# Context attention of a two-layer perceiver: the shifted queries are kept in the PSUM bank of the shift rows instead of in an SBUF tile

## The reference

```python
q = _ln((x @ Wq + bq).reshape(b, s1, H, HD), qn_w, qn_b)
k = _ln(kv[..., :HD], kn_w, kn_b);  v = kv[..., HD:]
ctx = _attn(qT, k.transpose(0, 2, 1, 3), v.transpose(0, 2, 1, 3))   # softmax(q k^T * SCALE) v over 1585 keys
ctx = ctx + DCA_WEIGHT * ctx_dca
return ctx @ Wo + bo
```

## Time and profile before

| | us |
|---|---|
| median of 3 runs (lowest to highest) | 3159.53 (3156.69 to 3160.48) |
| the profiled execution | 3156.05 |
| its span, first to last instruction | 3154.2 |
| PE busy | 2869.8 (91%) |
| DVE busy | 2625.1 (83%) |
| ACT busy | 2282.5 (72%) |
| POOL busy | 1615.4 (51%) |

### The profile page before, as it was taken

One profiled execution on the slowest core, in us unless ns is written; L12 is line 12 of the kernel. 1 busy time (PEld: TensorE's weight loads), 2 busy tenths in 40 slices (PEclk: granted clock), 3 DMA queues, 4 the chain that ended last, 5 costly groups with the idle time before them and its releaser, 6 DMA issues. The chain is left out here.

```text
span 3154.2 us, 87347 instructions
## 1 busy us (share of the span) xinstructions
PE 2869.8 (91%) x34089; PEld 1742.6 (55%) x34089; DVE 2625.1 (83%) x4082; ACT 2282.5 (72%) x4155; POOL 1615.4 (51%) x2006
## 2 busy tenths in 40 slices
PE   7689999999999878789996779999999999967889
PEld 3245555555555556577773325555555555555546
DVE  6699999999999756768875689999999999957752
ACT  5479999899899855346663459998999999873431
POOL 1257776776777642212223326777767776752210
PEclk9899999999999989889998899999999999988989
DMA  3344544454444344348894435544544444430020
GB/s 127 92 85 88 88 82 86 87 89 81 84 91 79 61 155 146 129 154 297 305 303 137 116 75 88 90 81 87 85 86 85 87 82 86 74 87 10 1 73 27
DMA packets 542690, 328.49 MB, mean 104 GB/s; under 512 B 459381, under 2 KB 504565, under 8 KB 536522
## 3 DMA queue, kind: packets, MB, share of 16 engines
q1 hardware_dynamic: 534314, 295.63, 40.8%
q0 software_dynamic: 7680, 25.17, 2.6%
q10 hardware_dynamic: 288, 2.10, 0.2%
HBM read 181.86 MB, written 36.09 MB: 69 GB/s over the span
## 5 line engine op out<-in xcount | busy, mean ns | idle before, releaser
L334 POOL TENSOR_TENSOR a_elo<-a_e 128x1024 f16<-128x1024 f32 x428 | 858.9, 2007 | 345.3 <-ACT a_e L421 343.4
L590 PE MATMUL a_ps_k<-l_wk,a_yh 128*128 128x512 f16 (+1 forms) x1664 | 571.0, 384 | 33.1 <-POOL a_yl L316 22.6
L590 PE MATMUL a_ps_v<-l_wv,a_yh 128*128 128x512 f16 (+1 forms) x1664 | 568.1, 382 | 11.5 <-DVE a_v L481 10.8
L492 DVE TENSOR_REDUCE a_mx<-a_ps_m 128x2 f32<-128x1024 f32 x384 | 467.3, 1217 | 7.0 <-PE a_ps_m L616 4.8
L419 ACT ACTIVATE a_e<-a_ps_t 128x1024 f32<-128x1024 f32 x428 | 408.9, 955 | 53.3 <-PE a_ps_t L650 51.1
L421 ACT ACTIVATE a_e<-a_ps_t 128x1024 f16<-128x1024 f32 x428 | 409.6, 957 | 0.4 <-PE a_ps_o L678 0.4
L650 PE MATMUL a_ps_t<-a_qb,a_kk 64*128 64x128 f16 (+1 forms) x9672 | 347.8, 218 | 41.3 <-DVE a_qb L516 32.1
L674 PEld LDWEIGHTS a_ps_o<-a_v,a_e 128*128 128x128 f16 (+1 forms) x3240 | 298.5, 96 | 118.4 <-issue 57.2
L674 PE MATMUL a_ps_o<-a_v,a_e 128*128 128x65 f16 (+1 forms) x3240 | 343.9, 193 | 18.4 <-POOL a_elo L334 18.3
L650 PEld LDWEIGHTS a_ps_t<-a_qb,a_kk 64*128 64x128 f16 (+1 forms) x9672 | 276.2, 95 | 128.8 <-issue 67.1
L676 PE MATMUL a_ps_o<-a_v,a_e 128*128 128x64 f16 (+1 forms) x3240 | 342.9, 194 | 0.0
(11 more groups left out here) (423 smaller groups left out, 5944.6 us busy)
## 6 DMA issues: line engine op xcount, KB each, us to landing
l_land<-in_ctx SPq DMA_DIRECT2D x96, 384.0 KB, 3.6
l_ob<-in_m_w SPq DMA_DIRECT2D x32, 1024.0 KB, 13.4
f_w<-in_m_w SPq DMA_DIRECT2D x32, 512.0 KB, 14.2
eo_dram<-f_e_eo SPq DMA_DIRECT2D x32, 512.0 KB, 4.3
l_land<-in_ctx SPq DMA_DIRECT2D x32, 433.0 KB, 3.9
a_kk<-a_khl SPq DMA_TRANSPOSE x416, 3.1
qs_dram<-p_q SPq DMA_DIRECT2D x32, 128.0 KB, 2.4
dca_dram<-p_od SPq DMA_DIRECT2D x16, 256.0 KB, 2.4
```

Source lines behind the costliest of these rows:

```text
L334: pool.tensor_tensor(rest[0:r, :, 0:w], full[0:r, :, 0:w], high[0:r, :, 0:w], ALU.subtract)\
L492: dve.tensor_reduce(mx[:, g, :, c], ps_m[:, :, :], AX.X, ALU.max).then_inc(mx_done, 1)
L590: m = pe.matmul(out[0:r, :], part[:, n % 2, c, cols], w[:, wpart, c, :], start=(c == 0 and a == 0), stop=(c == KC - 1 and a == 2))
```

## The change

The SBUF tile `q1` goes away. The name `q1` now stands for the first 256 columns of bank 0 of `ps_m`, where the shift rows lie: `qs` adds `q0` in place, and `qh` and `ql` read from there. DVE's own wait for `ql_done` before `qs` is dropped, and PE's `m0`, the next to write the bank, waits for `ql_done` instead of `q1_done`. The orders are unchanged.

```diff
-        q1 = sb("q1", [P, GROUPS, S])
...
+        q1 = ps_m[:, 0, 0:GROUPS * S].rearrange("p (g q) -> p g q", g=GROUPS)
...
-                        t = act.activation(qb[:, at.nbp, :, 0, a, :], q1[:, :, :], ACT.Copy, scale=mask[:, a:a + 1])
+                        t = act.activation(qb[:, at.nbp, :, 0, a, :], q1, ACT.Copy, scale=mask[:, a:a + 1])
...
-                    need(dve, ql_done, at.nb)
-                    dve.tensor_tensor(q1[:, :, :], ps_m[:, 0, 0:GROUPS * S].rearrange("p (g q) -> p g q", g=GROUPS),
-                                      q0[:, at.nbp], ALU.add).then_inc(q1_done, 1)
+                    dve.tensor_tensor(q1, q1, q0[:, at.nbp], ALU.add).then_inc(q1_done, 1)
...
-                        t = dve.scalar_tensor_tensor(out=qb[:, at.nbp, :, 1, a, :], in0=q1[:, :, :], scalar=mask[:, a:a + 1],
+                        t = dve.scalar_tensor_tensor(out=qb[:, at.nbp, :, 1, a, :], in0=q1, scalar=mask[:, a:a + 1],
                                                      in1=qb[:, at.nbp, :, 0, a, :], op0=ALU.mult, op1=ALU.subtract)
...
                     if m == 0:
                         pe.wait_ge(qm_done, at.nb + 1)
-                        need(pe, q1_done, at.nb)
+                        need(pe, ql_done, at.nb)
```

## The result

The changed kernel took 3122.3 us (median of 4 runs, 3115.8 to 3126.3) against 3158.1 for the kernel before beside it; the ratio is 0.9892, with a 95% interval of 0.9875 to 0.9909. The forecast was 3127.1 us, a ratio of 0.9897. The profiled execution took 3126.3 us, 29.8 less than the one of before.

The account below looks back on a forecast made before the run. PE was taken to bound context attention, waiting for `ql`. 28 middle batches x 1.15 us = 32.2, plus 0.2 for first batches, gave 3159.53 - 32.4 = 3127.1 us; range 3122 to 3133, 8 in 10 within 3121 to 3136.

Parts of the forecast that it names:

- What bounds the kernel: Context attention of both layers: PE busy about 58.9 of 60 us, waiting 32.1 us in 30 waits for `ql`.
- the sum: 28 middle batches at 1.15 us, 32.2, plus 0.2 for the two first batches; last batches zero; 32.4 us together.
- The hold: At `ql`, DVE instructions with two SBUF inputs wait for GpSimd's `lo12` and `yl3`; pair 2.63 us; `q1` in PSUM frees them.
- The rival that the mask column counts as a second input: At `ql`, the SBUF column keeps the pair at 2.63 us and the kernel at 3159.5 us; chance 4%.
- The loose reading: Skill page's contention rule at `ql`, with a pointer scalar not counted as an SBUF input; leads to 3127.1 us.
- The price of `ql`: DVE's two lower-part instructions a batch would last 0.97 us together, as in the first batch, instead of 2.63.
- The two bounds: For the `ql` pair: from below twice line 509's 0.42 us; from above twice 0.48, which is 0.96 us.
- the cover: At `s0`, the shifted queries would be ready 0.48 us before PE finishes the work ahead in its queue.
- PE's gain a batch: At `s0` PE gains 1.18 us; `k9` comes 0.03 late; 1.15 us counted for each middle batch.
- The next chain: POOL's `yl3`, shortened from 1.96 to 1.78 us, then PE's `k9` after 0.15 us of handover, 0.03 us late.
- `qh`, `qs`, the moved wait: ACT's upper part, DVE's shifted queries written to PSUM, and PE's new wait at `m0`: each counted as zero.
- The clock: Rival in both context attentions: pauseless PE has its clock fall to 1.2 GHz; 100 us of it gives 3177 us; 3%.

Follow-up runs that it names:

- two_psum: Changed kernel plus two idle VectorE instructions just ahead of `ql`, each with one input in PSUM and one in SBUF; ratio 0.9890 to the kernel before, median 3122.4 us.
- pause experiment: Changed kernel plus one idle GpSimd instruction of 32 columns ahead of `yl3`; ratio 0.9912 to the kernel before.
- one_sbuf: Changed kernel plus one idle VectorE instruction ahead of `ql` with both inputs in SBUF; ratio 0.9933 to the kernel before.
- again: The changed kernel as it is, measured again beside the kernel before; ratio 0.9892, median 3123.9 us of 5 runs.
- pool_order: The kernel before with `lo13` ahead of `yl3` in GpSimd's order; ratio 1.0136 to the kernel before.

## Why the prediction was right

*What bounds the kernel.* PE bound the stage and its one wait was `ql`. After the change that wait is gone from the middle batches and the stage's window shows PE busy throughout. What is left are two waits of 0.41 us, in the first batch of each layer, where it was 0.51: the 0.1 us each that the sum gave them.

*The hold.* Right, and shown rather than argued: two SBUF inputs beside a reading GpSimd instruction are held (2.63 us), one input in PSUM at the same place is not (0.75 us), two SBUF inputs beside an idle GpSimd are not (0.75 us). The rival that the mask column counts as a second input is refuted by 64 instructions of 473 to 484 ns, each with a column in SBUF, 60 of them with GpSimd busy beside them all along. The loose reading of the Trainium skill, page "SBUF — State Buffer", section "Who interferes with whom", is the one that holds here; a pointer scalar (the mask column) is no second input in its sense.

*The price of `ql`.* Taken at 0.97 us, measured 0.87. The pair of the first batch still contained a short hold of 0.10 us (0.576 and 0.472 us). The two bounds beside it, 0.84 and 0.96, doubled a single instruction, but two in a row overlap by 0.08 us: a pair of 0.42 lasts 0.75 us (`two_psum`) and a pair of 0.476 lasts 0.87. The single one, 0.48, was right. That 0.97 agreed with the upper bound was luck. It changed nothing, as the cover was 0.48 us and is 0.59 now (`s0` at 613.15; the pair ends at 612.50 and 0.06 passes).

*PE's gain a batch.* 1.18 forecast at `s0`, 0.03 given back at `k9`, 1.15 in all. Measured 60.40 - 59.23 = 1.17, and `k9` starts 0.80 us behind `s0` instead of 0.78: 0.02 given back. Times 28 this is 32.8 us.

*The next chain.* `yl3` ends at 613.80 and `k9` starts at 613.95, just the 0.15 us of the handover. The pause experiment shows that the chain is met exactly. That POOL would be sped up along with DVE carried 0.18 us of each batch; `one_sbuf` shows nearly this part by itself: `yl3` lasts 1.96 us again, `k9` comes 0.14 us later behind `s0`, and with 0.05 us at `s0` the period is 59.43.

*`qh`, `qs`, the moved wait.* `qh`'s two instructions of 466 ns take 0.83 us together where they took 0.90; `qs` went from a median of 414 ns to 422. The new wait at `m0` shows nowhere. (`m0` stands five steps behind `s0` in PE's queue, not six; nothing hangs on it.) In the median, moving the queries to PSUM made no instruction longer by more than 10 ns here.

*The clock.* Still 1.00 in the middle of the stage with PE busy at 100%.

*What the sum left out.* The profiled execution gained 29.8 us and not 32.4. The steady batches gave 32.8, the first ones 0.2, and the one long batch of the profile before another 0.9; five long batches of the profile after took back 5, and the rest of the kernel, which varies by more than that, gave 1 us. One of these waits, in PE's timeline:

```profile
469.32 0.39 PE L615 MATMUL a_ps_m<-a_kk,a_qm 64*128 64x512 f16 x2 [0.85 <-DMA a_kk<-a_khl]
```

`m8` needs the DMA transpose of key tile 11, which SP issues 3.8 us before `m8` starts in most batches. It lands 3.1 us after its issue there, 0.75 before it is needed; here it took 4.8. Neither the room nor the tail came with the change: the usual 0.75 us are the same in both kernels, and the transposes that took over 4.2 us from issue to landing are 49 and 51 of 416 in the two profiles of the kernel before, 49, 48 and 45 in the three of the changed one. Middle batches with a late tile 11 are 1 and 3 before, 5, 4 and 1 after. So the kernel before has them too; whether it has them as often, five profiles are too few to say.

It is not plain chance which tile is hit. Over the 12 profiles of all kernels here (384 transposes of each tile), tiles 8 and 10 are late 107 and 109 times, tile 5 74 times, tile 11 32 times and tile 9 never; in the ninth batch of layer 1 it is tile 11 in 7 of the 12 profiles. What decides this stays open.

The forecast is best compared with runs taken side by side. There the medians lie 35.8 us apart (4 and 4 runs) and 33.9 us in the round of `again` (9 and 5), both a little more than the 32.4 forecast. Late transposes and the rest of the kernel move single runs by several us, so an agreement closer than that is luck.

## What to carry to other kernels

The sign here was an instruction that lasted 1.5 to four times its shortest self (0.72 and 1.99 us against 0.47). When one does, look at what the other engine was running when it ended, and try one of its inputs where that engine doesn't read. The gain is the wait that it puts on the bounding engine (1.2 us a batch), not its own excess time (1.8 us), and the next chain should be worked out with its handover before one counts on it. Where a value passes through a PSUM bank that is free until the next stage, leaving it there saves the SBUF tile and this contention at no price seen here; the number of instructions stays the same.

## What the runs showed of the hardware that was not expected

A held VectorE instruction can be passed twice. In `pool_order` one waited from 622.2 us through two GpSimd instructions back to back and lasted up to 3.16 us, while in the kernel before, one that waited for `lo12` got its turn between `lo12` and `yl3` in all 28 middle batches.

The hold works both ways and the price is not the same: GpSimd's `yl3` lost 0.18 us (1.96 against 1.78) to VectorE instructions of 0.42 to 0.47 us, while these lost up to 1.5 us to it.

The DMA transposes have a long tail: 3.1 us in the median and over 4.2 us in 36 to 57 of 416, in every kernel here, and unevenly over the tiles (none of 384 for tile 9, 109 for tile 10). A hand-written order with 0.75 us of room for them pays about 1 us a hit, 1 to 5 times in the 28 middle batches.
